# Two cross-attention/FFN layers on one core: the last stage in seven tiles of 128 tokens instead of eight batches of 100

## The chip, the cores and the metric

The kernel runs on one core of one Trainium2 chip (trn2). The core's engines are TensorE (PE, with its weight loads shown apart as PEld), VectorE (DVE), ScalarE (ACT), GpSimd (POOL) and SyncE (SP, which here only issues transfers). The metric is the device time of one execution in microseconds. Three executions of the kernel before took 872.93, 882.98 and 877.28 us: median 877.28 us.

## The reference

Input is x (8 batches of 100 tokens, 512 wide) and a context (8 batches of 361 rows, 128 wide). Four residual steps follow each other:

```
x = x + L0_xattn(layernorm(x), ctx)   # 16 heads of 32, causal mask
x = x + L0_ffn(layernorm(x))          # 8 experts of 352, top 2
x = x + L1_xattn(layernorm(x), ctx)   # 16 heads, latent keys and values
x = x + L1_ffn(layernorm(x))          # 512 -> 2 x 1408 -> 512, quantised
```

The change is about the last two. In the second attention every head of a token has a query of 128 numbers (after folding weights into each other), and all heads share one set of 361 keys and values:

```
scores  = q_r . k_r          # 16 heads x 100 tokens rows per batch
attn    = softmax(scores)
ctx_c   = attn @ kv_rope     # 128 numbers for each token and head
out     = (ctx_c @ w_kc_kv per head, heads side by side) @ Wo.T
```

In the last FFN, activations and weights are rounded to 255 levels, the activations by a scale for each token (the row's largest magnitude / 127), the hidden vector of 1408 likewise:

```
xq = quant(layernorm(x)); gate, up = xq @ w1q.T split
h  = silu(gate) * up;     hq = quant(h);  y = hq @ w2q.T
```

No step mixes tokens except the softmaxes, so the last projection and the FFN may be cut anywhere along the 800 tokens.

## The kernel before, in words

The kernel is written by hand, one instruction stream per engine, with semaphores between them. What an engine does next is set by the order in which its stream is written; there is no planner. `B` is 8 batches, `T` is 100 tokens, `NH0` is 16 heads, `ROWS` is 1600 (token, head) rows per batch.

**float32 products in three passes.** Where full precision is wanted, an operand is split into a high part (`..._hi`, cast to fp32r) and a low part (`..._lo`, the difference), and `mm3` (lines 148 to 150) issues hi*hi, lo*hi and hi*lo. ACT makes the high part, DVE the low part.

**Second attention.** `queries_part` places the queries of two batches in `QH`/`QL`, `[128, batch, row]`, where a batch's row is head * 100 + token; ACT writes them with `act_queries` (line 876), DVE with `dve_queries` (line 1706). There are four such pairs of batches, with 12 steps each, of which the last 8 write `QH`/`QL`. A batch's 1600 rows are then worked through in 13 tiles: scores (PE), maximum (DVE), exponential (ACT), scaling (POOL, line 759), transposes (PE), and the product with the values (`P.V`), whose result `ctxo` (128 x 512 at a time) SP stores to `ctx_scratch` in DRAM (`store_ctx`, line 614).

**Last stage.** First PE folds the last two attention weights into `PF` (16 matmuls, line 1473, from `fp_raw`/`wraw`, loaded by `load_foldp`, line 602); ACT and DVE split it. Then for every batch n:

- `load_ctx` (line 635) brings the batch's context rows back as `cx_raw`, 128 x 1600, in two buffers; `split_ctx` (ACT, line 1053) and `low_ctx` (DVE, line 1892) split them into `cx_hi`, `cx_lo`;
- `project(n)` on PE: 16 heads x 3 matmuls of 512 columns, with `cx` as the stationary operand (128 x 100) and `PF` as the moving one;
- `add_out` (DVE, line 1903) adds the result to `X`, whose layout is `[100 tokens, batch, 512]`; statistics, normalising and quantising follow, and four transposes (`pe_xq`, line 1494), moved out by ACT as `xqt` (line 1073);
- `pe_gate_up`: 4 chunks of 8 bf16 matmuls of 352 columns (line 1505); DVE, ACT and POOL make h; 11 transposes (`pe_ht`, line 1514), moved out as `hqt` (line 1088) in two pieces; `pe_down`: 11 matmuls of 512 columns (line 1522);
- the result is added to `X` (POOL, line 792) and stored.

`pe_ffn(n)` interleaves these over batches. One pass works on the gate/up of n+1, the projection of n+3 and the down product of n; on ACT and DVE the split for n+4 lies in the same pass. Projections 0, 1 and 2 and gate/up 0 come before the first pass.

**The queue of SP** between the stages is, in this order: the last stores of `ctxo`, folded weights 2 and 3, `cx_raw` of batches 0 and 1, folded weights 4 to 7, then the FFN's weights `w1q` (2816 KB), `s_rows` (one row of 11 KB repeated over 100 partitions), `w2q` (1408 KB) and a second small `s_rows`, then `cx_raw` of batch 2 and on, each of which waits for the split of the batch that had its buffer. PE does not start gate/up 0 before all four FFN transfers have landed.

Of the kernel before, what the change touches and what calls it, by code (L numbers as in the profile page):

```python
# [8 lines left out]
F32 = mybir.dt.float32  # L9
F32R = mybir.dt.float32r  # L10
# [53 lines left out]
FP = DK + D  # L64

# [30 lines left out]
def build_kernel(nc, x, ctx_t, wq0_t, wkv0_t, wout0_t, ident_d, mask_d, wg_t, w12_d, w3_d, route_d,  # L96
                 ctxn_d, cos_d, sin_d, foldq_d, krt_d, foldp_d,
                 wup_d, wdown_d, wupt_d, wdownt_d, out):
    with ExitStack() as top:
# [52 lines left out]
        sb = sb_in(top)  # L152
        X = sb("X", [T, B, D])
# [6 lines left out]
        rstd = sb("rstd", [T, B])  # L160
        xn = sb("xn", [T, 2, D])
        route = sb("route", [T, RT_N])
# [150 lines left out]
        CXH = [sd(f"cx_hi{i}", [128, ROWS], F32R) for i in range(2)]  # L313
        CXL = [sd(f"cx_lo{i}", [128, ROWS], F32R) for i in range(2)]
# [3 lines left out]
        S1B = sd("s1_rows", [T, 2 * FI])  # L318
        S2B = sd("s2_rows", [T, D])
        CXR = [sd(f"cx_raw{i}", [128, ROWS]) for i in range(2)]  # L320
        XQ = [sd(f"xq{i}", [T, D], BF16) for i in range(2)]
        XQT = [sd(f"xqt{i}", [128, KC, T], BF16) for i in range(2)]
        sx = sd("sx", [T, 2, 3])
        sh = sd("sh", [T, 2, 4])
        hmx = sd("hmx", [T, 2, GC])
        GS = [sd(f"gs{i}", [T, GW_]) for i in range(2)]
        US = [sd(f"us{i}", [T, GW_]) for i in range(2)]
        HQT = [sd(f"hqt{i}", [128, IC, T], BF16) for i in range(2)]
        Y2 = [sd(f"y2_{i}", [T, D]) for i in range(2)]
        pd.close()  # L330
        H1 = [wraw[0:T, i * FI:(i + 1) * FI] for i in range(2)]
        HQ = [wraw[0:T, 2 * FI + i * FI // 2:2 * FI + (i + 1) * FI // 2].bitcast(BF16) for i in range(2)]
        FPR = fp_more + [wraw[:, i * 2 * FP:(i + 1) * 2 * FP].rearrange("p (h n) -> p h n", h=2) for i in range(2)]
        ctx_scratch = nc.dram_tensor("ctx_scratch", [B, 128, ROWS], F32, kind="Internal").ap()
# [21 lines left out]
        FFNW = C["kr"]  # L356
        YGS = [W[f"yg{i}"] for i in range(3)]
# [62 lines left out]
        HTG = [(0, 6), (6, IC)]  # L420
# [61 lines left out]
        def _(sp):  # L482
# [114 lines left out]
            load_kv(1, 1)  # L597
            def load_foldp(i):
# [11 lines left out]
            def store_ctx(n, g):  # L610
                cols = min(512, ROWS - g * 512)
                wait(sp, C["ctxo"], NG * n + g + 1)
                dst = ctx_scratch[n] if isinstance(n, int) else ctx_scratch[bass.ds(n, 1)].rearrange("o p r -> (o p) r")
                sp.dma_start(dst[:, g * 512:g * 512 + cols], ctxo[g % 2][:, 0:cols]).then_inc(C[f"st{g % 2}"], 16)
# [7 lines left out]
            with sp.Fori(0, B // 2 - 1) as p:  # L622
                store_batch(2 * p, 0)
                store_batch(2 * p + 1, 1)
# [1475 lines left out]
```

## Time and profile before

| | |
|---|---|
| median of 3 runs | 877.28 us (872.93 to 882.98) |
| the profiled execution's own time | 874.4 us |
| its span (first to last instruction) | 872.6 us |
| PE matmul busy | 732.0 us (84%) |
| DVE, ACT, POOL busy | 522.1, 424.2, 255.4 us |
| mean granted TensorE clock | 0.928 of full speed |
| second attention, roughly | 401 to 663 us |
| last stage, roughly | 663 to 872 us |

Times in the trace are counted from the start of the span. A timeline row gives an instruction's start, its length and, in brackets, how long its engine had stood idle before it and what ended that. The rows of one line of code are put together by the view by groups. The chain of waits shows which engine's work ended last at each moment. Matmul rows overlap, since the array is pipelined: the pace of a series is read from the distance between starts, not from their lengths.

### The profile page before, as it was taken

Reading aid. Unit: us, or ns where it says so; the run is one execution under the profiler, and the core shown is the slowest. Engines: PE = TensorE matmul, PEld = TensorE weight load, DVE = VectorE, ACT = ScalarE, POOL = GpSimd, SP = SyncE. Lnnn points to the kernel's source line nnn. Section 1 sums busy time; section 2 is a strip of 40 time slices with the busy share of each in tenths; the row PEclk is TensorE's granted clock in tenths of the full one; section 3 lists DMA queues with packets and bytes.
Section 4 is the critical chain, followed back from the end, with each engine's and each line's share of the span. In section 5 each row is a group of like instructions: output and inputs, shape, how many; then the busy total and the mean of one; then the engine's idle time right before and its main releaser. Section 6 shows DMA issues by size and latency. Waiting matters only on the chain.

```text
span 872.6 us, 13419 instructions
## 1 busy us (share of the span) xinstructions
PE 732.0 (84%) x4533; PEld 582.2 (67%) x4533; DVE 522.1 (60%) x1065; ACT 424.2 (49%) x790; POOL 255.4 (29%) x284
## 2 busy tenths in 40 slices
PE   0799998628999999965989989989986888999974
PEld 0597777517777777865878778778773455777752
DVE  4876675655666665256763664664663435777683
ACT  3523665345555554212674664664663314544552
POOL 1000931331222220332372461561640002222232
PEclk9997999658999999956999999999999899999997
DMA  8546632896675555772000110010015911110000
GB/s 265 198 166 216 238 105 84 319 343 220 201 233 182 169 179 165 252 208 69 1 34 27 35 45 25 22 46 24 17 45 217 347 69 45 57 57 10 11 19 19
DMA packets 51793, 108.71 MB, mean 125 GB/s; under 512 B 12149, under 2 KB 30321, under 8 KB 48953
## 3 DMA queue, kind: packets, MB, share of 16 engines
q1 hardware_dynamic: 48605, 99.50, 33.8%
q0 software_dynamic: 3136, 8.53, 3.8%
q8 instruction: 31, 0.51, 0.2%
q14 instruction: 21, 0.17, 0.1%
HBM read 88.59 MB, written 19.43 MB: 124 GB/s over the span
## 4 chain that ended last, share of the span: by engine, by line
PE 47%; issue 23%; DVE 10%; POOL 8%; DMA 5%; ACT 5%; ACTq 1%; SPq 0%; POOLq 0%; DVEq 0%
PE PS L148 10%; PE PS L150 9%; PE PS L149 9%; POOL wraw L759 5%; PE PS L1160 4%; PE PS L1505 3%; PE PS L1221 3%; PE PS L1522 2%; DMA raw<-wkv_in 1%; ACT w_hi L811 1%; DMA fq_raw<-foldq_in 1%; PE PS L1264 1%; PE PS L1204 1%; DMA fp_raw<-foldp_in 1%; DVE wscale L1760 1%
## 5 line engine op out<-in xcount | busy, mean ns | idle before, releaser
L759 POOL TENSOR_TENSOR wraw<-wraw,rinv 128x361 f32<-128x361 f32 (+1 forms) x104 | 80.8, 789 | 139.7 <-DVE rinv L1718 139.6
L1561 DVE TENSOR_TENSOR w_lo<-w,w_hi 128x1408 fp32r<-128x1408 f32 x40 | 64.8, 1620 | 40.1 <-ACT w_hi L811 40.1
L907 ACT ACTIVATE wraw<-PS,nmx 128x361 f32<-128x361 f32 (+1 forms) x104 | 58.6, 565 | 38.4 <-DVE nmx L1725 30.5
L1725 DVE TENSOR_REDUCE nmx<-PS 128x1 f32<-128x361 f32 (+1 forms) x104 | 55.0, 529 | 33.9 <-PE PS L150 33.7
L786 POOL TENSOR_TENSOR wraw<-gs,us 100x352 f32<-100x352 f32 x32 | 30.3, 947 | 152.3 <-ACT gs L1078 127.8
L711 POOL DMA_INDIRECT xb<-xn_scratch,rows x20 | 35.1, 1754 | 103.4 <-PE PS L1132 100.3
L811 ACT CAST w_hi<-w 128x1408 fp32r x40 | 54.7, 1370 | 18.8 <-issue 18.8
L148 PE MATMUL PS<-w_hi,xt_hi 128*128 128x352 f32 x160 | 56.8, 355 | 5.2 <-DVE xt_lo L1555 4.9
L148 PE MATMUL PS<-pf_hi,cx_hi 128*100 128x512 f32 x128 | 53.4, 418 | 8.9 <-DVE pf_lo L1896 3.7
L1728 DVE TENSOR_TENSOR pt_lo<-PS,pt_hi 128x384 fp32r<-128x384 f32 x96 | 52.2, 546 | 11.9 <-ACT pt_hi L913 11.1
L1320 PE MATMUL PS<-ident,wraw 128*128 128x128 f32 x312 | 52.1, 277 | 6.4 <-POOL wraw L759 4.2
L1160 PE MATMUL PS<-w,ht 128*128 128x512 f32 (+1 forms) x120 | 54.9, 593 | 0.7 <-DVE ht L1573 0.7
L150 PE MATMUL PS<-w_hi,xt_lo 128*128 128x352 f32 x160 | 52.5, 328 | 0.0
L149 PE MATMUL PS<-w_lo,xt_hi 128*128 128x352 f32 x160 | 52.4, 328 | 0.0
L1320 PEld LDWEIGHTS PS<-ident,wraw 128*128 128x128 f32 x312 | 37.6, 140 | 20.8 <-POOL wraw L759 10.1
L149 PE MATMUL PS<-pf_lo,cx_hi 128*100 128x512 f32 x128 | 50.9, 398 | 0.0
L150 PE MATMUL PS<-pf_hi,cx_lo 128*100 128x512 f32 x128 | 50.8, 397 | 0.0
L913 ACT CAST pt_hi<-PS 128x384 fp32r<-128x384 f32 x96 | 45.5, 476 | 6.2 <-PE PS L1320 6.2
L148 PE MATMUL PS<-kt_hi,q_hi 128*128 128x362 f32 (+1 forms) x104 | 42.6, 410 | 3.2 <-ACT wraw L907 1.6
L1505 PE MATMUL PS<-w1q,xqt 128*100 128x352 bf16 x256 | 44.0, 318 | 1.3 <-ACT xqt L1073 1.3
L148 PEld LDWEIGHTS PS<-w_hi,xt_hi 128*128 128x128 f32 x160 | 31.0, 194 | 18.5 <-DVE xt_lo L1555 18.5
L689 POOL TENSOR_TENSOR raw_even<-raw_even,wraw 128x384 f32<-128x384 f32 (+1 forms) x14 | 14.2, 1044 | 92.1 <-DMA inv_down<-sc_scratch 61.3
(277 smaller groups left out, 2036.9 us busy)
## 6 DMA issues: line engine op xcount, KB each, us to landing
w<-w_in SPq DMA_DIRECT2D x20, 768.0 KB, 5.4
w<-w_in SPq DMA_DIRECT2D x8, 1408.0 KB, 11.4
fq_raw<-foldq_in SPq DMA_DIRECT2D x6, 1088.0 KB, 7.9
cx_raw<-ctx_scratch SPq DMA_DIRECT2D x8, 800.0 KB, 5.5
ctx_scratch<-ctxo SPq DMA_DIRECT2D x24, 256.0 KB, 2.0
ys_scratch<-yb SPq DMA_DIRECT2D x20, 256.0 KB
wraw<-wup_in SPq DMA_DIRECT2D x12, 256.0 KB, 4.3
w1q<-w_scratch SPq DMA_DIRECT2D x1, 2816.0 KB
```

The source lines that it names most:

```text
L148: pe.matmul(o, lh, rh, start=start, stop=False)
L149: pe.matmul(o, lh, rl, start=False, stop=False)
L150: return pe.matmul(o, ll, rh, start=False, stop=stop)
L759: pool.tensor_tensor(P1[slot][0:rows, 0:NK], P1[slot][0:rows, 0:NK], rinv[0:rows, jj, t:t + 1].broadcast_to((rows, NK)), ALU.mult).then_in ...
L811: act.copy(WH[which][:, :], w12_of(act_whi.e, which)).then_inc(WHS[which], 1)
L907: act.activation(P1[t % 8][r, 0:NK], PS[r, t % 4, 0:NK], ACT.Exp, bias=nmx[r, jj, t:t + 1], accum_out=rsum[r, jj, t:t + 1]).then_inc(C["ex ...
L1160: last = pe.matmul(PS[:, 4 + i % 2, :], HT[i % 2][0:rows, c * 128:(c + 1) * 128], W3R[i % 2][0:rows, c * D:(c + 1) * D], start=(c == 0), s ...
L1320: last = pe.transpose(PS[:, 4 + t % 3, c * 128:(c + 1) * 128], P1[t % 8][:, c * 128:(c + 1) * 128], ident[:, :])
L1505: last = pe.matmul(PS[0:T, 2 * which + c % 2, 0:GW_], XQT[j][:, k, :], W1Q[:, k, at:at + GW_], start=(k == 0), stop=(k == KC - 1))
L1561: dve.tensor_tensor(WL[which][:, :], w12_of(dve_wlo.e, which), WH[which][:, :].bitcast(F32), ALU.subtract) \
L1725: dve.tensor_reduce(nmx[r, jj, t:t + 1], PS[r, t % 4, 0:NK], AX.X, ALU.max, negate=True).then_inc(C["max"], 1)
L1728: dve.tensor_tensor(pt_place(PTL, t, jj), turned(t), pt_place(PTH, t, jj).bitcast(F32), ALU.subtract) \
```

## The change

The last stage runs over `NTT` = 7 tiles of 128 tokens (`tokens(n)`: six times 128, then 32) that cross batch borders, where it ran over 8 batches of 100.

- `X` has to lie by tiles. SP stores it after the expert FFN to `x_scratch` in DRAM (8 stores) and, in the second attention after batch 5, loads it back as `XT` over the same memory.
- `QH`/`QL` are now ordered by token, then head, so that a tile of 128 tokens is one stretch of 2048 rows in `ctx_scratch`. ACT's and DVE's writes into them step over 16 elements (64 bytes) from one to the next.
- `cx_raw` is one buffer of 128 x 2048 in place of two of 128 x 1600. It comes in by token, then head, and `split_ctx`/`low_ctx` read it with a step of 16 elements, and write by head, then token.
- SP's queue: `load_ctx(1)` stands behind the folded weights and waits for the split of tile 0; the FFN's weights stand behind it.
- Tiles are up to 128 partitions high; the transposes come out in pieces of 7 and 4 instead of 6 and 5.

```
+NTT = -(-B * T // 128)
...
-        CXR = [sd(f"cx_raw{i}", [128, ROWS]) for i in range(2)]
+        CXR = sd("cx_raw", [128, 128 * NH0])
...
+        def tokens(n):
+            return min(128, B * T - 128 * n)
+        def by_head(t, n):
+            return t[:, 0:NH0 * tokens(n)].rearrange("p (h t) -> p h t", h=NH0)
+        def by_token(t, n):
+            return t[:, 0:NH0 * tokens(n)].rearrange("p (t h) -> p h t", h=NH0)
...
+            for b in range(B):
+                sp.wait_ge(E["x"], TOPK * (b + 1))
+                sp.dma_start(x_scratch[b * T:(b + 1) * T], X[:, b, :]).then_inc(XSTORED, 16)
...
+            sp.dma_start(XT[:, 0:full, :], x_scratch[0:128 * full].rearrange("(n p) d -> p n d", p=128)).then_inc(XLOADED, 16)
...
-                wait(sp, O["cxl"], n - 1)
+                wait(sp, O["cxl"], n)
...
             load_foldp(3)
-            load_ctx(0, 0)
-            load_ctx(1, 1)
+            load_ctx(0)
             for i in range(4, NP1):
                 load_foldp(i)
+            load_ctx(1)
...
-            o = (QH if hi else QL)[:, :, :].rearrange("p j (h t) -> p h j t", t=T)[:, h0:h0 + 3:2]
+            o = (QH if hi else QL)[:, :, :].rearrange("p j (t h) -> p h j t", h=NH0)[:, h0:h0 + 3:2]
...
-                act.copy(CXH[j][:, :], CXR[j][:, :]).then_inc(O["cxh"], 1)
+                act.copy(by_head(CXH[j], n), by_token(CXR, n)).then_inc(O["cxh"], 1)
...
-                dve.tensor_tensor(CXL[j][:, :], CXR[j][:, :], CXH[j][:, :].bitcast(F32), ALU.subtract).then_inc(O["cxl"], 1)
+                dve.tensor_tensor(by_head(CXL[j], n), by_token(CXR, n), by_head(CXH[j], n).bitcast(F32), ALU.subtract).then_inc(O["cxl"], 1)
...
-            for n in range(B):
+            for n in range(NTT):
                 pe_ffn(n, n % 2)
```

SP's queue between the stages, before (602 loads folded weights, 635 `cx_raw`, 644 to 647 the FFN's weights):

```order
L602 DMA wraw<-foldp_in 128x1280 x2
L635 DMA cx_raw<-ctx_scratch 128x1600 x2
L602 DMA fp_raw<-foldp_in 128x1280 x2
L602 DMA wraw<-foldp_in 128x1280 x2
L644 DMA w1q<-w_scratch 128x11264
L645 DMA s_rows<-sc_scratch 100x2816
L646 DMA w2q<-w_scratch 128x5632
L647 DMA s_rows<-sc_scratch 100x512
```

and after (639 loads folded weights, 675 `cx_raw`):

```order
L639 DMA wraw<-foldp_in 128x1280 x2
L675 DMA cx_raw<-ctx_scratch 128x2048
L639 DMA fp_raw<-foldp_in 128x1280 x2
L639 DMA wraw<-foldp_in 128x1280 x2
L675 DMA cx_raw<-ctx_scratch 128x2048
L685 DMA w1q<-w_scratch 128x11264
L686 DMA s_rows<-sc_scratch 128x2816
L687 DMA w2q<-w_scratch 128x5632
```

One load of `cx_raw` has moved behind six folded weights, and the FFN's weights stand behind it.

ACT in one pass of the last stage, before (1078 silu, 1088 the transposed h, 1053 the split, 1073 the transposed input):

```order
L1078 ACTIVATE gs<-gs 100x352
L1088 COPY hqt<-PS 128x600
L1088 COPY hqt<-PS 128x500
L1053 CAST cx_hi<-cx_raw 128x1600
L1078 ACTIVATE gs<-gs 100x352
L1073 COPY xqt<-PS 128x400
```

and after:

```order
L1117 ACTIVATE gs<-gs 128x352
L1129 COPY hqt<-PS 128x896
L1129 COPY hqt<-PS 128x512
L1089 CAST cx_hi<-cx_raw 128x2048
L1117 ACTIVATE gs<-gs 128x352
L1111 COPY xqt<-PS 128x512
```

The order is the same; three of the pieces are longer, and the split steps through its source.

## Rows read from the trace of the kernel before

**Rows 1.** Busy time by stretch (us; engines' busy us (instructions), TensorE clock, DMA share, GB/s)

```profile
560.00:580.00 20.00, 17.17 (x100) 14.03 (x100) 13.69 (x40) 14.07 (x42) 16.57 (x22) 1.00 0.07 26
760.00:780.00 20.00, 20.00 (x113) 14.48 (x112) 14.94 (x31) 10.54 (x14) 5.86 (x6) 1.00 0.17 53
```

**Rows 2.** The chain that ended last, steady passes: start us, us, what

```profile
754.71 2.38 PE PS L1522 x11
757.08 1.19 PE PS L1505 x8
...
773.63 2.38 PE PS L1522 x11
```

**Rows 3.** PE, P.V matmuls of the second attention: start us, us, instruction

```profile
660.71 0.39 PE L148 MATMUL PS<-pt_hi,kn_hi 128*128 128x512 f32 x1
660.94 0.40 PE L149 MATMUL PS<-pt_lo,kn_hi 128*128 128x512 f32 x1
```

**Rows 4.** ACT, then DVE, in the pass from 742 us, same columns [idle before]

```profile
751.39 1.54 ACT L1053 CAST cx_hi<-cx_raw 128x1600 fp32r<-128x1600 f32 x1
755.72 0.47 ACT L1073 COPY xqt<-PS 128x400 bf16<-128x400 bf16 x1
...
752.96 1.83 DVE L1892 TENSOR_TENSOR cx_lo<-cx_raw,cx_hi 128x1600 fp32r<-128x1600 f32 x1 [2.97 <-ACT cx_hi L1053]
```

**Rows 5.** Groups by line, shapes apart: busy us, mean ns of one | idle before

```profile
L932 ACT CAST hi<-raw 128x2048 fp32r<-128x2048 f32 x2 | 3.8, 1902 | 0.0
L1088 ACT COPY hqt<-PS 128x600 bf16<-128x600 bf16 x8 | 5.2, 653 | 10.4 <-PE PS L1514 10.4
...
L1754 DVE TENSOR_TENSOR lo<-raw,hi 128x2048 fp32r<-128x2048 f32 x2 | 4.6, 2280 | 0.0
...
L759 POOL TENSOR_TENSOR wraw<-wraw,rinv 128x361 f32<-128x361 f32 x96 | 74.6, 789 | 127.3 <-DVE rinv L1718 127.2
```

**Rows 6.** Same view: eight elements read 32 bytes apart, and eight side by side

```profile
L1589 DVE TENSOR_TENSOR probs<-top 100x8 f32<-100x8 f32 x1 | 0.2, 151 | 0.0
...
L1656 DVE TENSOR_TENSOR probs<-probs 100x8 f32<-100x8 f32 x1 | 0.2, 159 | 0.0
```

**Rows 7.** PE where it stands still at the head of the last stage

```profile
676.20 5.27 PE L1473 MATMUL PS<-fp_raw 128*128 128x512 f32 x8 [4.09 <-DMA fp_raw<-foldp_in]
...
688.58 0.48 PE L148 MATMUL PS<-pf_hi,cx_hi 128*100 128x512 f32 x1 [3.67 <-DVE pf_lo L1896]
...
718.38 0.45 PE L148 MATMUL PS<-pf_hi,cx_hi 128*100 128x512 f32 x1 [2.52 <-DVE X L1903]
...
739.12 0.48 PE L148 MATMUL PS<-pf_hi,cx_hi 128*100 128x512 f32 x1 [1.89 <-DVE cx_lo L1892]
```

**Rows 8.** ACT, then DVE, before the second of those three waits

```profile
714.25 1.53 ACT L1053 CAST cx_hi<-cx_raw 128x1600 fp32r<-128x1600 f32 x1
...
715.81 1.83 DVE L1892 TENSOR_TENSOR cx_lo<-cx_raw,cx_hi 128x1600 fp32r<-128x1600 f32 x1 [9.04 <-ACT cx_hi L1053]
717.56 0.68 DVE L1903 TENSOR_TENSOR X<-X,PS 100x512 f32<-100x512 f32 x1
```

**Rows 9.** DVE, then PE, at the end of the first pair's queries

```profile
425.67 1.04 DVE L1706 TENSOR_TENSOR q_lo<-PS,q_hi 128x400 fp32r<-128x400 f32 x2
...
426.76 0.65 PE L148 MATMUL PS<-kt_hi,q_hi 128*128 128x362 f32 x1 [1.41 <-DVE q_lo L1706]
```

**Rows 10.** SyncE's queue between the stages: start us, us from first to last issue

```profile
666.22 0.80 SPq L635 DMA_DIRECT2D cx_raw<-ctx_scratch  x2
...
672.52 0.43 SPq L644 DMA_DIRECT2D w1q<-w_scratch  x1
...
687.49 30.65 SPq L635 DMA_DIRECT2D cx_raw<-ctx_scratch  x3
```

**Rows 11.** Busy time and DMA by stretch, columns as in the first group

```profile
665.00:680.00 15.00, 9.55 (x18) 3.62 (x17) 6.22 (x9) 4.91 (x10) 0.00 (x0) 0.89 0.98 386
...
685.00:695.00 10.00, 6.42 (x21) 4.48 (x22) 5.25 (x5) 3.55 (x4) 0.00 (x0) 0.83 1.00 250
```

More of the change, by code:

```diff
@@ L320, in build_kernel @@
-        CXR = [sd(f"cx_raw{i}", [128, ROWS]) for i in range(2)]
[L321 to L329, printed above, removed]
@@ new lines, in build_kernel, with smalls @@
+        HQ = [wraw[:, 2 * FI + i * FI // 2:2 * FI + (i + 1) * FI // 2].bitcast(BF16) for i in range(2)]
+        small = wraw[:, 3 * FI:3 * FI + 12 * NTT + 22]
+        def smalls(at, *dims):
+            n = int(np.prod(dims))
+            v = small[:, at:at + n]
+            return v.rearrange("p (a b) -> p a b", a=dims[0]) if len(dims) == 2 else v
+        stats_e, mv_e = smalls(0, NTT, 6), smalls(6 * NTT, NTT, 2)
+        veps_e, std_e, rstd_e = (smalls((8 + i) * NTT, NTT) for i in range(3))
@@ L624, in _, with load_ctx @@
                 store_batch(2 * p + 1, 1)
+            sp.wait_ge(XSTORED, 16 + 16 * B)
+            sp.wait_ge(LN["xn"], 3 * B)
+            full = B * T // 128
+            sp.dma_start(XT[:, 0:full, :], x_scratch[0:128 * full].rearrange("(n p) d -> p n d", p=128)).then_inc(XLOADED, 16)
+            sp.dma_start(XT[0:tokens(full), full, :], x_scratch[128 * full:B * T]).then_inc(XLOADED, 16)
             store_batch(B - 2, 0, False)
             store_batch(B - 1, 1, False)
-            def load_ctx(n, j):
-                if isinstance(n, int) and n == 0:
+            def load_ctx(n):
+                if n == 0:
@@ L658, in _ @@
-            with sp.Fori(0, B // 2) as p:
-                store_out(2 * p, 0)
-                store_out(2 * p + 1, 1)
-            sp.wait_ge(OUTS[0], 16 * B // 2)
-            sp.wait_ge(OUTS[1], 16 * B // 2)
+            sp.dma_start(S2B[:, :], sc_scratch[0:1, 2 * FI:2 * FI + D].broadcast_to((128, D))).then_inc(FFNW, 16)
+            for n in range(2, NTT):
+                load_ctx(n)
+            rows_out = out.rearrange("b t d -> (b t) d")
+            for n in range(NTT):
+                wait(sp, F["res"], n + 1)
+                sp.dma_start(rows_out[128 * n:128 * n + tokens(n)], XT[0:tokens(n), n, :]).then_inc(OUTS[n % 2], 16)
@@ L790, in pool_add @@
                 wait(pool, F["y"], n + 1)
-                xs = X[:, n, :] if isinstance(n, int) else X[:, bass.ds(n, 1), :].rearrange("p a d -> p (a d)")
-                pool.tensor_tensor(xs, xs, Y2[j][:, :], ALU.add).then_inc(F["res"], 1)
+                r = tokens(n)
+                pool.tensor_tensor(XT[0:r, n, :], XT[0:r, n, :], Y2[j][0:r, :], ALU.add).then_inc(F["res"], 1)
             pool_h(0, 0)
-            for n in range(B):
-                if n + 1 < B:
+            for n in range(NTT):
+                if n + 1 < NTT:
                     pool_h(n + 1, (n + 1) % 2)
@@ L1123, in _ @@
             act_std(2)
-            for n in range(B):
+            for n in range(NTT):
                 act_ffn(n, n % 2)
@@ L1504, in pe_gate_up @@
                     for k in range(KC):
-                        last = pe.matmul(PS[0:T, 2 * which + c % 2, 0:GW_], XQT[j][:, k, :], W1Q[:, k, at:at + GW_],
+                        last = pe.matmul(PS[0:tokens(m), 2 * which + c % 2, 0:GW_], XQT[j][:, k, 0:tokens(m)], W1Q[:, k, at:at + GW_],
                                          start=(k == 0), stop=(k == KC - 1))
@@ L1548, in _ @@
             pe_xq(1, 1)
-            for n in range(B):
+            for n in range(NTT):
                 pe_ffn(n, n % 2)
@@ L2007, in _ @@
             low_ctx(3, 1)
-            for n in range(B):
+            for n in range(NTT):
                 dve_ffn(n, n % 2)
```

165 lines of the change are left out of this document (93 added, 72 removed).

## The prediction, made before the changed kernel was run

> **What bounds the kernel now.** I read the busy time by stretch first. In the last stage PE matmuls fill the stretch completely at full clock (20.00 of 20 us) while DVE has 14.94 and ACT 10.54; in the second attention no engine is full, PE is nearest (17.17 of 20), and DVE and ACT have 13.69 and 14.07 [rows 1]. Then the chain of waits in the last stage: down product, gate/up, projection follow each other on PE without a gap, and the down product comes again after 773.63 - 754.71 = 18.92 us [rows 2]. So a pass of the last stage costs 18.9 us of PE, and nothing else sets it. Third, PE's timeline at the head of the stage, where PE does stand still: 4.09 us for folded weights, 3.67 us for the low parts of `PF`, between whose last pieces ACT and DVE also split tile 0, 2.52 us for the chain of split 2, 1.89 us for split 3 [rows 7]. There ACT and DVE are the bound. Fourth, how near ACT and DVE come to being late in a full pass: the split on ACT from 751.39, the low part on DVE from 752.96, and `xqt` from 755.72 to 756.19, which gate/up at 757.08 needs [rows 2, 4]: 0.9 us to spare. Fifth, SP's queue and the DMA rate between the stages [rows 10, 11].
>
> **One pass less: -18.9 us.** Projections, gate/up and down products are counted by tile and not by token: their moving operands have 512 or 352 columns whatever the tile's height, and only the stationary operand grows from 100 to 128 columns. That this doesn't slow a matmul is seen in the second attention, where 512 columns against a stationary operand of 128 follow each other after 0.23 us [rows 3]. There are eight batches and five passes with a projection in them before; seven tiles and four such passes after. What leads in (projections 0 to 2) and what leads out (the last three tiles) stays as it is: the last tile, of 32 tokens, has the same column counts on PE.
>
> **Longer splits: +2.5 and +0.6 us.** 2048 columns in one piece take ACT 1902 ns and DVE 2280 ns [rows 5], against 1.53 and 1.83 us for 1600 now [rows 8]: together 0.8 us more. At tiles 0, 2 and 3 ACT and DVE work one after the other while PE stands [rows 7, 8], so 3 x 0.82 = +2.5 us. In a pass there is 0.9 us to spare. The split adds 0.8, `hqt` has 1408 columns instead of 1100 at about 1.1 ns (653 ns for 600) [rows 5], at most +0.3, and `xqt` 512 instead of 400, +0.1: 1.2 in all, so 0.3 us of PE comes to light in each of two passes (the splits of tiles 4 and 5): +0.6. The split of the small tile 6 has 512 columns and is shorter than before.
>
> **SP's queue: -1.5 and +1.6 us.** Ahead of the folded weights that PE waits 4.09 us for, there are now 1.05 MB of `cx_raw` instead of 2 x 0.82 MB; 0.59 MB at 386 GB/s [rows 11] is 1.5 us: -1.5. Then `load_ctx(1)` waits for the low part of tile 0. Before, a load with such a wait went out at 687.49 and the FFN's weights at 672.52 [rows 10]; now `cx_raw` 1, all four FFN transfers and, behind them, `cx_raw` 2 go out from about 686. That is 1.05 + 2.88 + 1.44 + 1.44 + 0.26 + 1.05 = 8.1 MB. At 386 GB/s it takes 21 us, at 250 GB/s, the rate of the stretch with the repeated rows, 32 us [rows 11]; half and half by bytes 26.7 us, and `cx_raw` 2 is there at about 714.3 (686 + 1.5 to begin + 26.7). ACT could use it at 714.25 - 1.5 = 712.7 [rows 8]: +1.6 us. The FFN's weights land some 3 us before that and just in time. Later loads have one buffer instead of two, but a pass between two of them.
>
> **X through DRAM: nothing.** The eight stores (1.6 MB) go out while the experts' results are added, ahead of two folded weights that are used only in the last stage. The load back falls into the second attention, where the DMA engines are 7% busy [rows 1]. If it held up a store of `ctxo`, the cost would be the load's own time, 1.5 MB at 386 GB/s, 4 us, once.
>
> **The step of 64 bytes: +16.4 us.** Without it the sum is -18.9 + 2.5 + 0.6 - 1.5 + 1.6 = -15.7. But ACT and DVE now step over 16 elements between two reads (`split_ctx`, `low_ctx`) or two writes (the queries). No long instruction of the trace does so. The bound below is nothing: eight elements read 32 bytes apart take 151 ns, side by side 159 ns [rows 6]; a gain is excluded, since the columns stay as many and no row shows them faster than side by side. But eight elements say little (1 ns each is 8 ns, as much as these two rows differ by). The bound above is the pace of POOL, which takes 789 ns for 361 columns, 2.19 ns each, where DVE takes (2280 - 1.83 us x 1000) / 448 = 1.0 ns and ACT 0.8 ns [rows 5, 8]: extra costs of 1.15 ns on DVE and 1.35 ns on ACT. Neither row is nearer in kind, so I take half: 0.58 ns on DVE, 0.67 ns on ACT. A split then costs 2048 x 1.25 ns = 2.6 us more. It shows at the three places where PE stands for it and in the two passes whose reserve is used up already: 5 x 2.6 = 12.8 us. In the attention a piece of 400 columns takes 0.23 us more on DVE and 0.27 us more on ACT. At the first pair DVE works through the eight query pieces and their neighbours without a pause and PE waits 1.41 us for the last [rows 9]: 8 x 0.23 + 0.27 = 2.1 us. At the other three pairs PE's own work spreads the pieces out, and the last piece's 0.5 us counts: 1.5 us.
>
> The Trainium skill speaks against this term being nothing. "Vector Engine (DVE) Microarchitecture Reference", section 5.2, says that a port keeps its full rate only while it meets at least two adjacent 4-byte words at a time, and measures 1.73 ns for a column with one source that hops at each element and up to 2.51 ns with steps of 24 words, against 1.05 ns. By an estimate from that page, with 0.68 ns more for a split's column on DVE, 0.95 ns for a query's and ACT untouched, the step would cost 7.0 us in the splits and 4.2 us at the queries, and the sum would be 870 us. The eight-element rows of this trace don't show the rule, and are too short to refute it.
>
> **Sum.** -15.7 + 16.4 = +0.7 against the profiled execution's own 874.4 us (its span 872.6 and 1.8 around it), so **875 us**. That execution was 2.9 us below the median of the three runs, 877.28, which themselves lie 10 us apart; 1% is 8.8 us, about what a measurement of this kernel can tell from no change.
>
> **Rivals.**
>
> - *The step is free.* For it: the eight-element rows. Then 874.4 - 15.7 = **859 us**. It would take both engines; if DVE alone pays half, it is 866.
> - *The step costs the whole bound, and the pass is given back with interest.* Each split costs 5.1 us, five of them 25.6, the queries 8 x 0.46 + 0.54 + 3 x 1.0 = 7.2: -15.7 + 32.8 = +17, **891 us**. Its place is between ACT's split and DVE's low part, one after the other while PE waits. One nanosecond of extra cost per column, over both engines together, is 13.1 us, so it is even at 1.2 ns, slower by 1% from 1.9 ns. For it: the two extra costs add up in series; against it: DVE and ACT are no POOL.
> - *The queue is the bound.* If 250 GB/s holds for all of the 8.1 MB, `cx_raw` 2 lands at 720 instead of 714 and the FFN's weights after PE needs them: +5.5 on the forecast, **881 us**. Against it: 386 GB/s just before, with rows of 5 and 22 KB as the weights have.
> - That PE keeps its passes but DVE becomes their bound is ruled out: 14.94 of 20 us is 14.1 in a pass, plus 0.5 for length and 1.2 for the step, 15.8 of 18.9.
>
> A longer standstill before projection 0 may also lower the clock: in the stretch from 685 to 695, after PE's wait of 3.67 us, it is at 0.83 of 2.4 GHz already, a part of it at 1.2 GHz: 1.7 us lost in 10 [rows 7, 11]. That much again is in the range.
>
> **How the numbers follow.** Forecast 0.45, its own range 869 to 882 (the step at 0.8 to 1.75 ns for both engines together). Free 0.24, whole bound 0.21, queue 0.10. Faster by over 1%: the free step and a twentieth of the forecast, 0.26. Slower by over 1%: the whole bound, a third of the queue and a twentieth of the forecast, 0.27. Within 1%: 0.47. The range reaches from a little below the free case to a little below the whole bound, 857 to 889.
>
> **What would show it.** Seven down products, four passes with a projection; in each of them PE full or short of it by what `xqt` is late. `cx_hi` of 128 x 2048 at 1.9 us (free), 3.3 us (half) or 4.7 us; `cx_lo` at 2.3, 3.5 or 4.6 us; a query piece of 400 columns at 0.49/0.57, 0.76/0.80 or 1.0/1.0 us. PE's wait before projection 2: 2.5 + 0.8 + 1.6 + 2.6 = 7.5 us by the forecast. The folded weights' wait at 2.6 instead of 4.09 us. Wrong it would be if the two halves of the price differ much, if the weights come later than the third tile's projection needs them, or if a pass's length changes for another reason than these.

## The result, and the profile after

The changed kernel takes **898.06 us** (median of 4 runs, 896.31 to 901.72) against 878.88 us for the kernel before in the same session (4 runs): ratio 1.0242, 95% interval 1.0200 to 1.0283. It is slower, and 9 us beyond the range's upper end. The profiled execution took 901.72 us with a span of 899.9.

The page of the changed kernel, section 2: the granted clock in tenths, in 40 slices of 22.5 us.

```profile
PEclk9897997859999999758898898899799798899997
```

In the page of before the 20th to the 31st slice are all 9, through the second attention. Now six of the 20th to the 29th are 8 or 7: the attention itself runs at a lower clock, which no step of the prediction had.

Groups by line, shapes apart (busy us, mean ns of one | idle before): the splits of the last stage, to be held against [rows 5], and the pieces of the attention's queries.

```profile
L1089 ACT CAST cx_hi<-cx_raw 128x2048 fp32r<-128x2048 f32 x6 | 22.1, 3678 | 8.2 <-DMA cx_raw<-ctx_scratch 8.2
L1936 DVE TENSOR_TENSOR cx_lo<-cx_raw,cx_hi 128x2048 fp32r<-128x2048 f32 x6 | 21.8, 3632 | 33.3 <-ACT cx_hi L1089 33.3
L912 ACT CAST q_hi<-PS 128x400 fp32r<-128x400 f32 x32 | 25.6, 868 | 14.3 <-PE PS L151 14.3
L1750 DVE TENSOR_TENSOR q_lo<-PS,q_hi 128x400 fp32r<-128x400 f32 x32 | 26.9, 876 | 22.2 <-ACT q_hi L912 22.1
```

Against 1902 and 2280 ns side by side [rows 5], a stepped split costs ACT 1.78 us and DVE 1.35 us more: 0.87 and 0.66 ns a column, 1.53 together, where I took 1.25.

PE's timeline where it stands still at the head of the last stage; answers [rows 7].

```profile
697.58 5.35 PE L1514 MATMUL PS<-fp_raw 128*128 128x512 f32 x8 [2.22 <-DMA fp_raw<-foldp_in]
713.95 0.79 PE L149 MATMUL PS<-pf_hi,cx_hi 128*128 128x512 f32 x1 [7.59 <-DVE pf_lo L1940]
...
747.82 0.77 PE L149 MATMUL PS<-pf_hi,cx_hi 128*128 128x512 f32 x1 [6.42 <-DVE x_tiles L1950]
...
774.60 0.80 PE L149 MATMUL PS<-pf_hi,cx_hi 128*128 128x512 f32 x1 [5.81 <-DVE cx_lo L1936]
798.39 1.37 PE L1548 MATMUL PS<-w1q,xqt 128*128 128x352 bf16 x8 [3.38 <-ACT xqt L1111]
```

Projections 0, 2 and 3 wait 3.9 us longer each, and gate/up now waits for `xqt` in two passes (821.05 has a second 3.37).

At the first pair's queries PE waits 2.95 us, 1.5 us longer than the 1.41 of [rows 9]:

```profile
429.45 0.67 PE L149 MATMUL PS<-kt_hi,q_hi 128*128 128x362 f32 x1 [2.95 <-DVE q_lo L1750]
```

In each of the three later pairs there is one place at which it now stands longer. This is PE's timeline there for the first two of them, in the kernel before (first fence) and after.

```profile
483.61 0.47 PE L148 MATMUL PS<-pt_hi,kn_hi 128*128 128x512 f32 x1 [0.36 <-DVE pt_lo L1728]
546.44 0.47 PE L148 MATMUL PS<-pt_hi,kn_hi 128*128 128x512 f32 x1 [0.37 <-DVE pt_lo L1728]
```

```profile
487.74 0.47 PE L149 MATMUL PS<-pt_hi,kn_hi 128*128 128x512 f32 x1 [1.33 <-DVE pt_lo L1772]
...
556.60 0.47 PE L149 MATMUL PS<-pt_hi,kn_hi 128*128 128x512 f32 x1 [1.35 <-DVE pt_lo L1772]
```

One microsecond more. What follows it is seen in the busy time by stretch (columns as in [rows 1]: the stretch, then PE, PEld, DVE, ACT and POOL, then the granted clock), before and after:

```profile
488.00:496.00 8.00, 7.35 (x46) 6.21 (x45) 5.23 (x15) 5.07 (x16) 3.24 (x5) 1.00 0.19 60
496.00:504.00 8.00, 6.88 (x42) 5.34 (x41) 6.26 (x18) 6.67 (x21) 8.00 (x11) 1.00 0.01 2
```

```profile
488.00:496.00 8.00, 8.00 (x29) 5.80 (x29) 3.15 (x5) 2.60 (x4) 0.00 (x0) 0.58 0.01 2
496.00:504.00 8.00, 8.00 (x35) 7.80 (x34) 4.03 (x11) 3.92 (x11) 2.81 (x4) 0.57 0.19 60
```

After the standstill at 486.4 PE is granted mostly 1.2 GHz, half of its full clock, for some 13 us. It looks fully busy (8.00 of 8) and does 29 matmuls where it did 46. (The same work lies 4.1 us earlier in the kernel before; its stretch from 484 to 492 us holds 49.) That is how such a fall shows: busy time up, count down.

SyncE's queue gives the length of a pair: the first of each pair's stores of `ctxo`, after.

```profile
446.36 15.43 SPq L650 DMA_DIRECT2D ctx_scratch<-ctxo  x4
...
515.16 15.47 SPq L650 DMA_DIRECT2D ctx_scratch<-ctxo  x4
...
584.38 15.42 SPq L650 DMA_DIRECT2D ctx_scratch<-ctxo  x4
```

68.80 and 69.22 us; before they are 443.16, 506.06 and 568.90, so 62.90 and 62.84.

A wait of that length does not lower the clock everywhere. These are two waits at other places of the kernel before, which the changed kernel has as well, and the stretches behind them, with the clock at 1.00:

```profile
577.23 0.47 PE L148 MATMUL PS<-pt_hi,kn_hi 128*128 128x512 f32 x1 [1.04 <-DVE pt_lo L1728]
...
658.88 0.50 PE L148 MATMUL PS<-pt_hi,kn_hi 128*128 128x512 f32 x1 [1.46 <-DVE pt_lo L1728]
```

```profile
576.00:584.00 8.00, 6.61 (x43) 5.61 (x42) 4.61 (x13) 5.62 (x19) 4.90 (x6) 1.00 0.17 64
656.00:664.00 8.00, 5.82 (x33) 4.39 (x32) 1.94 (x4) 2.95 (x7) 0.00 (x0) 1.00 0.18 66
```

The attention's last matmuls start at 662.29 before and 685.23 now (+22.9), and the last stage behind them has 210.3 and 214.7 us (+4.4).

### The profile page after: what moved, and what is told of

Same layout as the page of the kernel before. It is cut to its first block, busy times and chain, and to the rows that moved or that the text cites. A ratio compares the mean times of both kernels' runs of the same rounds, so it can differ in the third digit from the quotient of the medians.

```text
span 899.9 us, 13091 instructions
## 1 busy us (share of the span) xinstructions
PE 737.4 (82%) x4421; PEld 582.5 (65%) x4427; DVE 528.6 (59%) x1037; ACT 438.4 (49%) x777; POOL 250.8 (28%) x279
## 4 chain that ended last, share of the span: by engine, by line
PE 52%; DVE 14%; issue 14%; ACT 9%; DMA 6%; POOL 3%; ACTq 1%; SPq 0%; POOLq 0%; DVEq 0%
PE PS L149 13%; PE PS L151 11%; PE PS L150 11%; PE PS L1201 3%; PE PS L1262 3%; PE PS L1548 3%; ACT cx_hi L1089 2%; POOL wraw L794 2%; ACT w_hi L847 2%; PE PS L1361 2%; DMA raw<-wkv_in 1%; DMA fq_raw<-foldq_in 1%; DVE cx_lo L1936 1%; PE PS L1305 1%; PE PS L1245 1%
## 5 line engine op out<-in xcount | busy, mean ns | idle before, releaser
L822 POOL TENSOR_TENSOR wraw<-gs,us 128x352 f32<-128x352 f32 (+1 forms) x28 | 26.6, 950 | 164.3 <-ACT gs L1117 133.5
L149 PE MATMUL PS<-pf_hi,cx_hi 128*128 128x512 f32 (+1 forms) x112 | 49.3, 440 | 20.7 <-DVE pf_lo L1940 7.6
L149 PE MATMUL PS<-kt_hi,q_hi 128*128 128x362 f32 (+1 forms) x104 | 45.2, 435 | 4.6 <-DVE q_lo L1750 3.0
L1548 PE MATMUL PS<-w1q,xqt 128*128 128x352 bf16 (+1 forms) x224 | 39.8, 326 | 8.2 <-ACT xqt L1111 8.2
L150 PE MATMUL PS<-pf_lo,cx_hi 128*128 128x512 f32 (+1 forms) x112 | 46.0, 410 | 0.0
L151 PE MATMUL PS<-pf_hi,cx_lo 128*128 128x512 f32 (+1 forms) x112 | 46.0, 410 | 0.0
L149 PE MATMUL PS<-pt_hi,kn_hi 128*128 128x512 f32 x72 | 33.2, 460 | 13.6 <-DVE pt_lo L1772 13.5
L1936 DVE TENSOR_TENSOR cx_lo<-cx_raw,cx_hi 128x2048 fp32r<-128x2048 f32 (+1 forms) x7 | 22.8, 3261 | 36.1 <-ACT cx_hi L1089 36.1
```

The source lines that it names most:

```text
L149: pe.matmul(o, lh, rh, start=start, stop=False)
L150: pe.matmul(o, lh, rl, start=False, stop=False)
L151: return pe.matmul(o, ll, rh, start=False, stop=stop)
L1548: last = pe.matmul(PS[0:tokens(m), 2 * which + c % 2, 0:GW_], XQT[j][:, k, 0:tokens(m)], W1Q[:, k, at:at + GW_], start=(k == 0), stop=(k = ...
```

## The experiments

**Theory:** all of the loss is the 64-byte step. It lengthens the splits in the last stage, and in the attention it makes PE stand 1 us longer once in a pair, which lowers the clock. **Rivals:** the X transfers or the new DRAM layout slow the attention; late pieces cost only their own length; the clock fell for another cause. Each kernel's ratio is to the kernel before, run beside it.

**1 to 3. The step taken back, in the queries, in the splits, in both.** The column order is the only edit; the instructions and their sizes stay. (In all three the last stage multiplies columns of the context by another head's weights; that the rows "stand in another order", as two of the expectations put it, is too little. "Every eighth column", there and in 6, 7 and 10, should be every sixteenth, and "projections 0, 1 and 2", there and in 10 and 11, should be 0, 2 and 3.)

```diff
-            o = (QH if hi else QL)[:, :, :].rearrange("p j (t h) -> p h j t", h=NH0)[:, h0:h0 + 3:2]
+            o = (QH if hi else QL)[:, :, :].rearrange("p j (h t) -> p h j t", t=T)[:, h0:h0 + 3:2]
```

```diff
-            return t[:, 0:NH0 * tokens(n)].rearrange("p (t h) -> p h t", h=NH0)
+            return t[:, 0:NH0 * tokens(n)].rearrange("p (h t) -> p h t", h=NH0)
```

> The changed kernel with one thing taken back: the two halves of the second attention's queries are written in the old order (a head's 100 tokens side by side) instead of every eighth column. Everything behind them is left as it is, so the rows of the output stand in another order. Theory (the 64-byte step makes the query pieces late, the tensor engine stands once in each pair, and its clock then falls to 1.2 GHz for some 13 us): the attention ends about 663 us into the span as before, not 686, the granted clock in the windows behind each pair's start is 1.00 again, q_hi is back at 0.49 us and q_lo at 0.57, and the time is 898 - 23 = 875 us. Rival one (X through DRAM, the new layout of the context, or its stores slow the attention): no change, 898. Rival two (only the engines' own added time counts, 0.37 + 0.31 us a piece, and the clock fell for another reason): the low windows stay, 894 us.

> The changed kernel with the last stage's splits reading the loaded context side by side instead of every eighth column; the queries keep their new order, so the products are taken over mixed columns and the time alone is to be read. Theory (the step makes each split 1.76 us longer on the scalar engine and 1.35 us on the vector engine, and the tensor engine stands for it at three places before projections 0, 1 and 2): cx_hi 1.90 us, cx_lo 2.28, the waits before the projections 7.6, 6.4 and 5.8 us shrink by 3 to 4 us each, the last stage is 9 to 14 us shorter: 884 to 889 us. Rival (the splits wait for loads that come late, and the step lies behind them): the waits before projections 1 and 2 stay, 1 to 3 us at most: 896. The attention is the same as in the changed kernel either way, with its low clock.

> Both edits at once: no 64-byte step is left anywhere, the rest of the change stays (seven passes of 128 tokens, X through DRAM, fold weights earlier); the rows of the output stand in another order. Theory (the step is all that was against the change): the gains of the two kernels beside it add up, 898 - 23 - 11 = 864 us, 1 to 2% under the kernel before. Rival (the seven passes themselves lose, through the longer pair loads and standstills at the projections): 875 or more, no faster than before.

| kernel | median us (runs) | ratio, 95% interval | attention's last matmuls | last stage us |
|---|---|---|---|---|
| queries by head | 878.66 (10) | 1.0009, 0.9978 to 1.0039 | 666.67 | 215.1 |
| splits by head | 876.52 (10) | 0.9988, 0.9961 to 1.0015 | 679.08 | 194.3 |
| both | 859.91 (4) | 0.9790, 0.9750 to 0.9830 | 663.30 | 195.0 |

The step in the queries costs 19.4 us, in the splits 21.5 (18.8 against the first), both 38.2: the two steps are more than the whole loss. X through DRAM and the layout stay in the third kernel, and its attention ends within 1 us of before. Part of the spread between 21.5 and 18.8 may be pairs without a long fall of the clock (the second kernel's trace has one); in the last stage alone the split's step is 20.4 us (214.7 against 194.3) and 20.1 (215.1 against 195.0). The waits of the third kernel:

```profile
688.42 0.66 PE L149 MATMUL PS<-pf_hi,cx_hi 128*128 128x512 f32 x1 [4.51 <-DVE pf_lo L1940]
...
718.97 0.47 PE L149 MATMUL PS<-pf_hi,cx_hi 128*128 128x512 f32 x1 [3.37 <-DVE x_tiles L1950]
...
742.25 0.50 PE L149 MATMUL PS<-pf_hi,cx_hi 128*128 128x512 f32 x1 [2.75 <-DVE cx_lo L1936]
```

Against 3.67, 2.52 and 1.89 [rows 7] these are 0.84 to 0.86 us more, the longer splits as forecast (0.82); against 7.59, 6.42 and 5.81 they are 3.05 to 3.08 less, the step. The two waits for `xqt` fall from 3.38 and 3.37 to 0.28 each (0.3 was forecast without the step). But the 0.85 us more has a price in clock as well. Before and in the third kernel:

```profile
720.00:740.00 20.00, 15.87 (x82) 11.31 (x82) 11.81 (x24) 8.37 (x11) 3.77 (x4) 1.00 0.06 26
740.00:760.00 20.00, 20.00 (x113) 14.50 (x112) 14.94 (x30) 10.61 (x15) 5.11 (x6) 1.00 0.25 83
```

```profile
720.00:740.00 20.00, 17.17 (x82) 12.09 (x80) 9.73 (x22) 6.77 (x10) 3.77 (x4) 0.93 0.11 47
740.00:760.00 20.00, 17.75 (x90) 13.11 (x91) 12.70 (x21) 9.73 (x11) 2.82 (x3) 0.91 0.15 52
```

Behind waits of 2.52 and 1.89 us the clock was 1.00; behind 3.37 and 2.75 it is not. I had expected 9 to 14 us from the splits: among other things I left out the two waits for `xqt`, though the prediction had counted those passes.

**4. A version for use.** Queries stay by head; the context lies in DRAM by head, then token of all batches, so the transfers do the reordering.

```diff
-        ctx_scratch = nc.dram_tensor("ctx_scratch", [128, B * ROWS], F32, kind="Internal").ap()
+        ctx_scratch = nc.dram_tensor("ctx_scratch", [128, NH0, B * T], F32, kind="Internal").ap()
...
-                sp.dma_start(CXR[:, 0:NH0 * tokens(n)], ctx_scratch[:, 128 * NH0 * n:128 * NH0 * n + NH0 * tokens(n)]) \
+                sp.dma_start(by_head(CXR, n), ctx_scratch[:, :, 128 * n:128 * n + tokens(n)]) \
```

> A version for use: seven tiles of 128 tokens, but queries stay ordered by head then token; the context lies in DRAM by head and then by token of all batches, so that a tile of 128 tokens is read as eight pieces of 512 bytes a partition, and each store of a group of rows is cut into up to three by head. No step on any engine. Theory (the order can be changed by the transfers for nothing): as the kernel with both edits, 864 us, the first split waiting at most 1 us more. Rival (pieces of 400 to 512 bytes load slower than 4 KB, or the nine stores a batch hold SP's queue): the load of cx_raw takes some 3 us more and the last stage 3 to 9 us, 867 to 873.

862.75 us (4 runs), ratio 0.9815 (0.9773 to 0.9856): the gain of both edits but for 3 us (the intervals overlap), nearer the theory (864) than the rival (867 to 873). The expectation miscounted the pieces: there are 16 heads, so 16 pieces a partition.

**5. The late pieces alone, in the kernel before.**

```diff
+            again = [4, 5, 6]
+            if k in again and not isinstance(q, int):
+                dve.tensor_tensor(o, bank, hi.bitcast(F32), ALU.subtract).then_inc(C["dup"], 1)
+                wait(dve, C["dup"], len(again) * (q - 1) + again.index(k) + 1)
             dve.tensor_tensor(o, bank, hi.bitcast(F32), ALU.subtract).then_inc(C["prl"], 1)
```

> The kernel before, with no 64-byte step, no X through DRAM and the old last stage; alone, in each of the three later pairs the vector engine computes the low half of three query pieces (the fifth to the seventh of the twelve, 0.57 us each) twice, so that the pt_lo behind them comes some 1.2 to 1.7 us later. The output is the same. Theory (it is enough that the tensor engine stands once for a late pt_lo, whatever made it late): the wait before the pair's fourth group of P.V grows from 0.36 us to 1.3 us or more, the granted clock then falls to 0.5 for some 13 us, and each pair costs 5 to 7 us more: 877.8 + 18 = 896 us. Rival (the lateness costs its own length, and the clock fell in the changed kernel through the stepped accesses or the layout): clock 1.00 there, 1 to 1.5 us a pair, 881 us.

("Fourth group" is a slip here and in the next three expectations: it is the third group of P.V of the pair's second batch.) 899.5 us, ratio 1.0252 (1.0173 to 1.0330). PE and the stretches behind it:

```profile
484.16 0.47 PE L148 MATMUL PS<-pt_hi,kn_hi 128*128 128x512 f32 x1 [1.82 <-DVE pt_lo L1732]
```

```profile
484.00:492.00 8.00, 7.84 (x25) 5.43 (x25) 2.39 (x5) 1.30 (x3) 0.00 (x0) 0.55 0.01 2
492.00:500.00 8.00, 8.00 (x35) 7.80 (x35) 2.88 (x9) 3.39 (x10) 1.65 (x2) 0.60 0.19 60
```

A kernel with nothing of the change has the changed kernel's attention: three pieces a pair, each computed twice (0.57 us), lengthen PE's wait by 1.5 us and cost 25.6 us on 873.9. The rival (881) falls.

**6 and 7. One half stepped at a time** (high half stepped, low by head, and the reverse).

```diff
-            o = (QH if hi else QL)[:, :, :].rearrange("p j (t h) -> p h j t", h=NH0)[:, h0:h0 + 3:2]
+            o = QH[:, :, :].rearrange("p j (t h) -> p h j t", h=NH0)[:, h0:h0 + 3:2] if hi else \
+                QL[:, :, :].rearrange("p j (h t) -> p h j t", t=T)[:, h0:h0 + 3:2]
```

> The changed kernel, but only the high halves of the queries are written at every eighth column (the scalar engine's write, and the vector engine's read of it); the low halves are written side by side. The products mix columns, so only the time counts. Theory (two engines add their lateness on one path, q_hi +0.37 us and q_lo +0.31): q_hi 0.87 us, q_lo between 0.57 and 0.88; the wait before the fourth P.V stays between 0.7 and 1.3 us; if it is under about 1 us the clock may hold, 880 us, otherwise 890 to 898. Rival (the scalar engine's write is hidden, since it is the vector engine that the tensor engine waits for): q_hi 0.87, wait as in the kernel before, 879 us.

> The changed kernel, but only the low halves of the queries are written at every eighth column (the vector engine's write alone); the high halves are written and read side by side. The products mix columns, so only the time counts. Theory: q_hi 0.49 us, q_lo 0.6 to 0.88, the wait before the fourth P.V between 0.5 and 1.1 us, and the clock by whether that is long enough: 880 us if it holds, 890 or more if not. Rival (the vector engine pays for the stepped read and not for the stepped write): q_lo 0.57 us, wait 0.4, 879 us.

High half: 895.89 us, ratio 1.0232 (1.0145 to 1.0319). Low half: 884.80, ratio 1.0115 (1.0050 to 1.0180). Their `q_lo`, each first of its kernel:

```profile
L1751 DVE TENSOR_TENSOR q_lo<-PS,q_hi 128x400 fp32r<-128x400 f32 x32 | 25.7, 830 | 19.4 <-ACT q_hi L913 19.2
```

```profile
L1751 DVE TENSOR_TENSOR q_lo<-PS,q_hi 128x400 fp32r<-128x400 f32 x32 | 25.3, 842 | 10.6 <-ACT q_hi L913 10.3
```

DVE pays the same for a stepped read alone (830 ns) and a stepped write alone (842), nearly as much as for both (876; none 569). PE's wait and the time of a pair, over the traces:

| wait of PE at that group | kernels | clock behind it | pair, us |
|---|---|---|---|
| 0.36 | before, queries by head | 1.00; in the pair of 63.9 a short fall (0.81 from 557 to 565 us) | 62.7 to 62.9, one 63.9 |
| 0.77 | low half stepped | 1.00; in the third pair a short fall (0.79 from 621 to 629 us) | 63.5, 63.5, 63.9 |
| 1.25 to 1.36 | changed, high half stepped | long fall in five pairs of six | 68.8 to 70.2; the sixth 64.8 |
| 1.81 | kernel before, pieces twice | long fall in all three | 69.7 to 70.6 |

**8 and 9. Filling the standstill.** Six products of finished keys into the bank that the group then overwrites; in the first kernel at the batch's first group, by my mistake, in the second (`g == 2`) at the third.

```diff
+                        if kind == "odd" and dn == 0 and g == 0:
+                            for _ in range(6):
+                                pe.matmul(PS[:, 7, 0:LK * DK], KNH[jj][:, 0, :], KNH[jj][:, :, :].rearrange("p c d -> p (c d)"),
+                                          start=True, stop=True)
```

> The changed kernel with its 64-byte steps left as they are, and work added: ahead of the wait for pt_lo at the fourth group of P.V of each later pair, the tensor engine multiplies six times 128 x 384 columns of finished keys (some 0.17 us each at full clock, 1.1 us in all) into the bank that the group then overwrites. The output is the same. Theory (the standstill and not the length of the pieces costs the 20 us, through the clock): the wait falls from 1.35 to about 0.3 us, the clock stays 1.00 behind it, and the kernel with more work is faster: 898 - 15 to 18 = 880 to 883 us. Rival (the clock falls for another reason, or the time goes to the late pieces themselves): 898 or a little more.

> The kernel before this one had its six extra products ahead of the pair's first group of P.V, where the tensor engine did not stand; they ran at 462 to 600 us and the wait of 1.25 us stayed at the third group (of the pair's second batch). Here the same six (334 ns each in that trace, three behind one another a good 0.5 us, so 1.0 us in all) stand ahead of the third group, at the standstill itself; the 64-byte steps are left as they are and the output is the same. Theory (the standstill lowers the clock, and the clock costs the time): the wait falls from 1.35 to about 0.3 us, the windows behind it are granted 1.00, a pair takes 63.5 us again instead of 68.8, and the kernel is 15 to 18 us faster than the changed one: 880 to 883 us. Rival (the clock falls for another reason than the standstill): 895 or more with the low windows in place.

In the wrong place: 895.46 us, the wait still 1.25, the clock still low; it serves as the control for added products as such, and for the order of PE's waits, which both edits change alike. In the right place **886.51 us** (885.17 to 887.33), ratio 1.0129 (1.0061 to 1.0197), 11.6 us under the changed kernel (10 by the two ratios) with its steps untouched. PE there, and the stretches behind:

```profile
483.79 1.34 PE L1372 MATMUL PS<-kn_hi 128*128 128x384 f32 x6
485.04 0.51 PE L149 MATMUL PS<-pt_hi,kn_hi 128*128 128x512 f32 x1
```

```profile
488.00:496.00 8.00, 7.33 (x39) 6.59 (x39) 4.50 (x9) 4.21 (x10) 1.15 (x2) 0.83 0.19 60
496.00:504.00 8.00, 7.02 (x42) 5.67 (x40) 6.25 (x19) 7.21 (x23) 8.00 (x12) 0.96 0.00 1
```

The wait is gone and the fall is short, not absent. Pairs take 64.5 to 64.7 us instead of 68.8 to 70.1. Together with number 5, which makes the long fall by a longer standstill alone, this shows that the standstill causes it. Between the two profiled executions the gain is 16.6 us (899.9 against 883.3), within the 15 to 18 expected; the medians are probably nearer because the changed kernel doesn't fall in every pair of every run, which only a trace of those runs could show.

**10. Only the split's high half stepped** (`by_head(CXR, n)` for DVE's source).

> The changed kernel; of the last stage's splits only the high half (scalar engine) reads the context at every eighth column, the low half (vector engine) reads it side by side. The products mix columns, so only the time counts. Theory (both halves lie one behind the other on the path, the scalar engine has 1.76 us of the step and the vector engine 1.35): cx_hi 3.68 us, cx_lo 2.28, the waits before projections 0, 1 and 2 shrink by 1.35 us each from 7.6, 6.4 and 5.8, and the xqt waits of passes 3 and 4 of 3.4 us go at least in part: 3 x 1.35 and what the clock gives back, 888 to 893 us. Rival (the vector engine waits for the scalar engine's next split anyway): no change at the projections, 896 us.

886.25 us, ratio 1.0132 (1.0060 to 1.0204). `cx_lo` 2291 ns; the five waits are 6.27, 5.10, 4.31, 2.05 and 2.05 us, each 1.3 to 1.5 shorter. The last stage is 10.6 us shorter (204.1 against 214.7). The attention of the profiled execution is shorter too, since one of its pairs (65.3 us) has no long fall. The two engines' costs lie one behind the other in all five places; the rival falls.

**11 to 15. The last stage kept busy.** Extra products into an unused bank ahead of the projections; numbers 12 and 14 on the changed kernel, 11, 13 and 15 on the version for use. The cut below is that of 12 and 14 for projections 2 and 3; those ahead of projection 0 (16 in number 12, 8 in number 14) are the same loop on folded weights that are already there.

```diff
+                    for _ in range({2: 26, 3: 23}.get(n, 0)):
+                        pe.matmul(PS[:, 7, :], PFH[:, 0, 0:128], PFH[:, 0, :], start=True, stop=True)
                     wait(pe, O["cxl"], n + 1)
```

> The version with the context in DRAM by head, and ahead of projections 0, 1 and 2 of the last stage, where its tensor engine stood 4.5, 3.4 and 2.8 us, 8, 12 and 10 extra products of 128 x 512 columns into a bank that is not yet in use. The output is the same. Theory (the windows of 0.83 behind these standstills are their price in clock): the granted clock from 680 to 760 us is 1.00, and some 20 us at 0.83 to 0.91 give back 2 to 4 us: 862.75 - 3 = 860 us. Rival (what runs at the low clock there waits for the splits anyway): 863 us, or 1 to 2 us more where a standstill is overfilled.

> The changed kernel with its steps and its order of the queries as they are; ahead of projections 0, 2 and 3 of the last stage, where the tensor engine stands 7.6, 6.4 and 5.8 us, it gets 16, 26 and 23 extra products of 128 x 512 columns (0.44 us each before the first, 0.235 before the others: 7.0, 6.1 and 5.4 us) into a bank not yet in use. The output is the same. Theory (of the 20 us that the stepped splits cost, 15 are the standstills themselves and some 5 the clock behind them): the splits end as late as before, the windows at 714 to 728, 742 to 756 and 770 to 784 us rise from 0.86, 0.76 and 0.76 to 1.00, and the last stage takes 209 to 211 us instead of 214.7: 893 to 894 us. Rival (behind each standstill the tensor engine only runs ahead to the next one, and its pace does not matter): 214 to 215 us, 898 us.

> The version with the context in DRAM by head, with extra products ahead of projections 0, 2 and 3 (9, 13 and 11), where it stood 4.5, 3.4 and 2.8 us. In the kernel with extra products shown before, the second group of twelve stood ahead of projection 1, which waits only 0.87 us, and the third was one projection early. The output is the same. Theory (there 2 us of work on the path had been added, against 3 to 4 us that the clock gave back): without them the clock is 1.00 from 690 to 760 us and the time 2 to 3 us under the version without extra products: 860 us. Rival (the pace of these windows does not set the end): 863 us.

> As the changed kernel with its projections kept busy, but 8 extra products ahead of projection 0, not 16: the trace of that run has two records of 0.44 us for each, so 16 of them took 14 us where 7.6 were free, and projection 0 began at 714.33 us though its last pf_lo was done at 708.75. With 8, projection 0 begins within 0.3 us of that operand. The output is the same. Theory (the clock behind the standstills costs some 5 us in this stage): the last stage takes 215.7 - 5.4 = 210.3 us or a little more, 4 us under the changed kernel's 214.7: 894 us. Rival (what the clock gives back at one place is waited for at the next, where the tensor engine then stands longer for xqt and its clock falls there): 213 to 215 us, 897 us.

> The version with the context in DRAM by head, kept busy ahead of projections 0, 2 and 3 by 5, 13 and 11 extra products. With 9 ahead of projection 0 it began 2.7 us after its last operand was done (688.74 against 686.03 us), and the median was 860.68. Theory: projection 0 begins 2.7 us earlier and everything behind it too, 858 us, the fastest of all. Rival (the early part is waited for later, at the context's or the weights' loads): 860 to 861 us.

| number | median us (runs) | ratio, 95% interval |
|---|---|---|
| 11, two groups misplaced | 862.80 (4) | 0.9870, 0.9796 to 0.9945 |
| 12, first group too long | 899.30 (6) | 1.0213, 1.0151 to 1.0275 |
| 13, first group too long | 860.68 (6) | 0.9810, 0.9770 to 0.9850 |
| 14, sized | 891.12 (6) | 1.0163, 1.0110 to 1.0215 |
| 15, sized | **856.75** (6) | 0.9779, 0.9732 to 0.9826 |

Number 12 looked like the rival's win, but its trace showed that its 16 products ran 5.6 us beyond their operand (projection 0 at 714.33, its last `pf_lo` done at 708.75). With 8 (number 14) the projection starts almost at once, and the last stage takes 888.7 - 680.5 = 208.2 us against 214.7: 6.5 us of that stage had been clock (0.86, 0.76 and 0.76 from 714, 742 and 770 us over 14 us each in the changed kernel). Number 14's head of the stage:

```profile
706.98 0.50 PE L149 MATMUL PS<-pf_hi,cx_hi 128*128 128x512 f32 x1 [0.79 <-DVE pf_lo L1945]
...
786.21 1.40 PE L1553 MATMUL PS<-w1q,xqt 128*128 128x352 bf16 x8 [3.38 <-ACT xqt L1111]
```

The rival has a part of the truth: behind the wait at 786.21, which was not filled, the clock is 0.88 from 784 to 798 us; behind the same wait of the changed kernel, at 798.39, it is 1.00 from 798 to 812. Number 15 has the lowest median of all, 2.2% under the kernel before. Against the version for use without the products that is 6.0 us by medians and 3 by ratios, and the two ratios' intervals overlap; its last stage is 4.8 us shorter (192.8 against 197.6).

## Why the prediction was wrong

- **The step that failed is "In the attention a piece of 400 columns takes 0.23 us more on DVE and 0.27 us more on ACT ... the last piece's 0.5 us counts: 1.5 us".** The lengths were near (measured +0.31 and +0.37 us), and the first pair's wait went from 1.41 [rows 9] to 2.95 us, +1.5 for my 2.1. The other three pairs were forecast at 1.5 us together and took 18.7 (446.36 to 654.52 against 446.52 to 635.99 with the queries by head; 19.8 against 444.21 to 632.60 of the kernel with both edits). I charged PE for the wait and not for what PE is granted after it. The prediction names this mechanism, but only for projection 0 and only with 1.7 us in the range. The same omission holds for the last stage, where it puts nothing for the clock behind the waits before projections 2 and 3. It would have needed one question more: where in the attention does PE already wait a little (0.36 us, in no row of mine), and does that wait grow? Even that would have given the suspicion and not the price: waits of 1.04 and 1.46 us elsewhere leave the clock at 1.00.
- **The splits' term, 12.8 us, was mis-sized.** The five places were right. Each costs 3.05 to 3.10 us, not 2.6: 15.4 us. The last stage lost 20.1 to 20.4 by the step. The 5 us that remain are mostly the clock behind the same standstills: filling three of them gave 6.5 us back, though some of that was lost before the change too (0.83 in [rows 11]).
- **Without the step the forecast was -15.7; measured -14.3** (spans of the profiled runs, 858.3 against 872.6) and -17.8 by medians. The nearness is in part luck, since two misses cancel. The longer splits held to 0.04 us a place. The wait for the last folded weights fell from 4.09 to 2.22 us (forecast 2.6). `cx_raw` 2 late, +1.6, did not show: the wait before projection 2 without the step is 3.37, which is 2.52 and the longer split. Against that stands the clock behind the longer waits, 0.93 and 0.91 from 720 to 760 us where it had been 1.00, which the forecast put at nothing. With these waits and the one before projection 0 filled (number 15) the last stage takes 192.8 us, 17.5 less than before, and the sum without the late `cx_raw` was -17.3. X through DRAM shows no cost: the attention ends at 663.30 against 662.29.
- **The rival "whole bound", 891, had the right side and the wrong reason.** Per column the step cost 1.53 ns, not 2.5.
- **On DVE the skill was nearer than half of POOL's extra price (0.58 ns, measured 0.66).** A stepped split takes DVE 3632 / 2048 = 1.77 ns a column. The Trainium skill, "Vector Engine (DVE) Microarchitecture Reference", section 5.2, gives 1.73 for one source that hops at each element. The eight-element rows [rows 6] had shown none of it. ACT, which I had let half a POOL price stand for, pays more (0.87 ns).

**Open:** why a wait of 1.3 us at this place makes the clock fall for long in most pairs and not in all, why waits of 1.04 to 2.52 us at some other places of the kernel before leave it at 1.00, and how the splits' cost divides exactly between the standstills (15.4) and the clock.

## What to carry to other kernels

Before a late operand is priced at its length, ask what the granted clock does behind the standstill, and test it at that very place: here one microsecond more of waiting on PE cost some six a pair, waits as long elsewhere did not lower the clock, and six throwaway products in place of the wait gave most of the loss back. A layout whose step falls on a compute engine is paid per column and on each engine in the chain; the same reordering in the DRAM side of a transfer that runs anyway cost 3 us here. A filler must be sized from a trace of the filler itself.

## What the runs showed of the hardware that I had not expected

- DVE pays for a step once: read alone 830 ns, write alone 842, both 876, none 569, for 400 columns. ACT pays 374 ns for a stepped write of 400 columns and 1.78 us for a stepped read of 2048, 0.93 and 0.87 ns a column.
- At the third P.V group of a pair's second batch, waits of 1.21 to 1.36 us are at the edge: of 21 such pairs in seven traces, 15 show the long fall (68.3 to 70.2 us) and 6 do not (64.8 to 65.3). That is probably why the runs of one kernel lie some 5 us apart (884.8, 890 to 894 for number 14); only one run of each kernel has a trace.
- A product of 128 x 512 in f32 takes two records of 0.44 us (number 12: 32 records for 16 products, 13.90 us); one in fp32r takes a single record, and they follow each other after 0.23 us.
